# A third raw buffer for the weights' maxima, the last head's sums on another engine, a weight tile rounded one stage earlier, and a new order in the first head

## Chip, cores, metric

One core of one Trainium2 chip. The time is device microseconds of one execution, the median over runs. Engines: TensorE (PE), VectorE (DVE), ScalarE (ACT), GpSimd (POOL), and SyncE (SP), whose queue issues all DMAs here.

## What is computed

A gated layer of two parts. The first ("mixer") adds to x a convolution over the sequence of the products of a context with itself, times the LayerNorm of x. The second is a feed-forward net of two linear layers whose operands are rounded to 8-bit integers with one exponent per block of 32.

```python
def xattn(k, v, q, ssm_kernel, D):           # k = v = the context, q = layernorm(x); head_dim 8, 64 heads
    kv = einsum('bhil,bhjl->bijhl', k_, v_)
    y = irfft(rfft(kv, 2 * L) * rfft(ssm_kernel, 2 * L))[..., :L]
    return einsum('bijhl,bhil->bjhl', y + kv * D, q_)

def mx_quant(x):                             # blocks of 32 along the contraction
    scale = exp2(floor(log2(amax)) - 6)
    return clip(round(xb / scale), -128, 127) * scale

def ffn(x):                                  # weights W1 (4096 x 1024), W2 (1024 x 4096)
    h = bf16(layernorm(bf16(x)) * w + b)
    h = gelu(bf16(mx_quant(h) @ mx_quant(W1).T + b1))
    return bf16(bf16(x) + bf16(mx_quant(h) @ mx_quant(W2).T + b2))

x = x + tanh(g_xattn) * xattn(ctx, ctx, layernorm(x), ssm_kernel, D)
x = x + tanh(g_ffn) * ffn(layernorm(x))
```

x is 8 x 512 x 1024: 32 tiles of 128 rows by 1024.

## The kernel before

The program has two blocks, one behind the other, with all engines meeting between them: `mixer_block` and `ffn_block`. Every order is written out by hand, engine by engine; semaphores tie them.

**First stage.** It runs over 64 heads, two to a tile (`TILE_HEADS`). For a head, ACT copies k (`copy_k`), writes its squares (`squares`) and the upper part of the products in reduced precision (`high_half`, kk_hi); DVE makes the products (`make_kk`) and the rest (`low_half`, kk_lo). TensorE convolves in stretches (`conv_stretch`, L307) with slabs of the taps, which SP loads for each head from a scratch in memory. At the start of a head TensorE waits for kk_lo of that head. DVE multiplies the result with q (`times_q`, in two parts, three instructions each); POOL sums the products in seven adds (`sum_part`, L709 to L721). Once per tile TensorE turns the sums back (`turn_back`, L340), DVE adds x (`residual`, L621), and SP stores the tile (`store_x1`). In the other direction ACT normalises x (`ln_apply`), TensorE turns it (`turn_q`, L320) and ACT takes it (`take_q`).

Between these, DVE takes the maxima of blocks of both weights (`weight_maxima`, L579): 32 tiles of 1 MB, one in each of the first heads, then in alternate heads, and from head 21 on three in two heads (`maxima_heads`). They are loaded by `load_w` into two raw buffers. From head 35 on DVE rounds the second layer's weights (`layer2_ints`, `layer2_clip`, `layer2_quant`) and SP stores them. In the heads between, the first four tiles of the second stage are prepared (`early_*`).

At its end SP waits for all its stores, the last tile's too, before the block ends (L286 to L288).

**Second stage.** The 16 tiles of W1 are loaded (`load_raw`, four buffers; tile 0 is already loaded by `first_loads`), and DVE rounds each in four steps: `weight_ints` (L1159 conversion, L1161 scale), `weight_clip` (L1166), `weight_quant` (L1171). Each releases one bank of the first layer on TensorE (`layer1`, L922). The tiles of x go in groups of two (g): first layer, bias on ACT (`add_bias`, L981), gelu (L988), the rounding of the hidden values on DVE (`peak`, `hidden_*`), second layer (`layer2`, L937), then `second_bias` (L1139, L1142) and `gated_sum` (L1148) on DVE and the store. Banks of group 1 begin eleven banks behind those of group 0. ACT's queue holds `first_norm` of group g + 2 ahead of `add_bias` of group g + 1, and `norm_again` within it, which waits for a tile of x that SP reloads (`reload`) behind the store of the tile before.

## Time and profile before

| what | us |
|---|---|
| median of 3 runs | 2006.51 (2004.93 to 2008.56) |
| the profiled execution, its own time | 2008.35 |
| its span | 2006.4 |
| TensorE busy | 1904.8 (95%) |
| DVE busy | 1694.4 (84%) |
| POOL busy | 962.3 (48%), nearly all in the first stage |
| ACT busy | 755.7 (38%) |

The span is what the rows below measure; the execution's own time holds 1.95 us more around it. Times in the rows are microseconds from the span's start. The stages change near 1028 to 1054 us.

### The profile page before, as it was taken

To read this page: it belongs to the slowest core of one execution; us is meant where nothing else is said; L and a number is where in the kernel's file an instruction comes from. 1 tells how busy PE (TensorE), PEld (TensorE's weight loads), DVE (VectorE), ACT (ScalarE), POOL (GpSimd) and SP (SyncE) were. 2 spreads that over 40 slices of the span, in tenths; PEclk is the share of its full clock that TensorE was granted. 3 is DMA by queue.
4 is the path that set the end of the run, shared out by engine and by line. 5 is a ranking of instruction groups with operands and counts; after the bars stand their busy time and mean duration, and the time that the engine had idled before them with its cause. 6 is when DMAs were issued, how large, how long until landed. Compare 5 with 4: busy or idle time off the path is not lost. (4 is left out here: it accounts for less than half of the span.)

```text
span 2006.4 us, 29505 instructions
## 1 busy us (share of the span) xinstructions
PE 1904.8 (95%) x11680; PEld 1499.5 (75%) x11680; DVE 1694.4 (84%) x2075; ACT 755.7 (38%) x1036; POOL 962.3 (48%) x1035
## 2 busy tenths in 40 slices
PE   6999999999999999999955969999999999999998
PEld 5988888888888898889843736667676666666673
DVE  6899999998898889898859799888888888898843
ACT  3333333333333433333302604444444444444440
POOL 4888899887899999999960000000000000000000
PEclk9999999999999999999978979999999999999999
DMA  6544545555554655555438411222221212212111
GB/s 245 192 171 155 169 157 181 199 213 213 213 199 137 204 181 171 193 181 195 147 112 327 178 49 58 64 74 74 74 74 64 60 57 74 74 54 64 53 43 74
DMA packets 99274, 271.75 MB, mean 135 GB/s; under 512 B 41472, under 2 KB 41472, under 8 KB 90944
## 3 DMA queue, kind: packets, MB, share of 16 engines
q1 hardware_dynamic: 99136, 269.86, 39.3%
q8 instruction: 92, 1.51, 0.3%
q14 instruction: 46, 0.38, 0.1%
HBM read 218.91 MB, written 42.53 MB: 130 GB/s over the span
## 5 line engine op out<-in xcount | busy, mean ns | idle before, releaser
L307 PE MATMUL y_ps<-kk_hi,slab 128*128 128x352 f32 (+6 forms) x3328 | 896.9, 351 | 15.5 <-issue 10.6
L307 PEld LDWEIGHTS y_ps<-kk_hi,slab 128*128 128x128 f32 x3328 | 595.7, 189 | 85.7 <-issue 12.1
L307 PE MATMUL y_ps<-kk_lo,slab 128*128 128x512 f32 (+6 forms) x1664 | 580.7, 349 | 0.0
L937 PE MATMUL acc_ps<-w_T,arena 128*128 128x512 bf16 x2048 | 444.5, 379 | 0.0
L922 PE MATMUL l_ps<-f_xq_T,w_T 128*128 128x256 bf16 x3584 | 398.9, 275 | 19.3 <-ACT arena L981 14.7
L922 PEld LDWEIGHTS l_ps<-f_xq_T,w_T 128*128 128x128 bf16 x3584 | 352.8, 99 | 66.3 <-ACT arena L981 15.2
L937 PEld LDWEIGHTS acc_ps<-w_T,arena 128*128 128x128 bf16 x2048 | 200.4, 98 | 238.4
L1221 POOL TENSOR_TENSOR f_rstd<-f_var_eps,f_neg_half 128x1 f32<-128x1 f32 x28 | 15.4, 549 | 707.3 <-DVE f_var_eps L1037 707.3
L307 PEld LDWEIGHTS y_ps<-kk_lo,slab 128*128 128x128 f32 x1664 | 314.1, 189 | 34.4
L981 ACT ACTIVATE arena<-l_ps,f_b 128x256 bf16<-128x256 f32 x512 | 213.7, 474 | 237.8 <-PE l_ps L922 232.8
L495 DVE TENSOR_TENSOR upper<-y_ps,q_ext 128x768 f32<-128x768 f32 (+1 forms) x128 | 155.8, 1217 | 79.8 <-PE y_ps L307 74.2
L709 POOL TENSOR_TENSOR lsum<-lower 128x240 f32<-128x240 f32 (+1 forms) x128 | 159.1, 1243 | 73.2 <-DVE lower L501 73.1
L367 ACT COPY k_ps<-k_ext 128x512 f32<-128x512 f32 x64 | 37.8, 591 | 412.6 <-DVE kk L475 405.1
L710 POOL TENSOR_TENSOR upper<-upper 128x384 f32<-128x384 f32 (+1 forms) x128 | 185.2, 1447 | 0.0
L481 DVE TENSOR_TENSOR kk_lo<-kk,kk_hi 128x2304 fp32r<-128x2304 f32 x64 | 174.1, 2721 | 10.6 <-ACT kk_hi L381 10.1
L721 POOL TENSOR_TENSOR mixed<-upper 128x192 f32<-128x192 f32 (+1 forms) x128 | 168.7, 1318 | 18.6 <-POOL upper L718 0.4
L381 ACT CAST kk_hi<-kk 128x2304 fp32r<-128x2304 f32 x64 | 136.2, 2128 | 7.9 <-DVE kk L475 5.9
L962 ACT ACTIVATE f_n<-arena,f_shift,f_rstd 128x1024 bf16<-128x1024 f32 x28 | 34.6, 1240 | 247.8 <-POOL f_shift L1223 247.8
L988 ACT ACTIVATE arena<-arena 128x2048 bf16<-128x2048 bf16 x64 | 122.0, 1911 | 0.5
L501 DVE TENSOR_TENSOR lower<-y_ps,q_ext 128x576 f32<-128x576 f32 (+1 forms) x128 | 121.0, 945 | 0.0
L712 POOL TENSOR_TENSOR lsum<-lsum,lower 128x240 f32<-128x240 f32 (+1 forms) x128 | 120.4, 941 | 0.0
L472 DVE TENSOR_TENSOR kk<-k_ps,k_ext 128x1536 f32<-128x1536 f32 x64 | 111.6, 1744 | 0.0
(125 smaller groups left out, 2062.7 us busy)
## 6 DMA issues: line engine op xcount, KB each, us to landing
slab<-taps_scratch SPq DMA_DIRECT2D x128, 512.0 KB, 4.8
arena<-in_w_m SPq DMA_DIRECT2D x32, 1024.0 KB, 6.4
arena<-x_scratch SPq DMA_DIRECT2D x60, 512.0 KB, 4.0
k_ext<-in_ctx_e SPq DMA_DIRECT2D x64, 384.0 KB, 3.5
arena<-in_w SPq DMA_DIRECT2D x17, 1024.0 KB, 7.1
x_tile<-in_x_t SPq DMA_DIRECT2D x32, 512.0 KB, 6.3
x_scratch<-x SPq DMA_DIRECT2D x32, 512.0 KB, 4.5
out_t<-arena SPq DMA_DIRECT2D x32, 512.0 KB, 2.6
```

The costliest lines, as they stand in the source:

```text
L307: mm = nc.tensor.matmul(y_ps[:, y_base + begin:y_base + end], slab[s][:, half, d * P:(d + 1) * P], kk_part[s][:, begin - d * PAIR:end - d ...
L381: nc.scalar.copy(kk_hi[h % 2][:], kk[:].rearrange("p n c -> p (n c)")).then_inc(hi_ready, 1)
L481: nc.vector.tensor_tensor(kk_lo[h % 2][:], kk[:].rearrange("p n c -> p (n c)"), kk_hi[h % 2][:].bitcast(F32), ALU.subtract).then_inc(lo_re ...
L495: nc.vector.tensor_tensor(view(up, 0, [((DIAG + 1) * CH, count), (CH, DIAG), (1, CH)]), view(y_ps, y_at, [(PAIR, count), (CH, DIAG), (1, C ...
L501: nc.vector.tensor_tensor(view(low, B, [(3 * ACCW, count), (ACCW + B, 3), (1, CH)]), view(y_ps, y_at + CH, [(PAIR, count), (CH, 3), (1, CH)]),
L709: add(lsum[:, :, B:], low[:, :, 0, B:], low[:, :, 1, B:], ALU.add).then_inc(lower_two, 1)
L710: add(up[:, :, 0:2, :], up[:, :, 0:2, :], up[:, :, 2:4, :], ALU.add).then_inc(upper_two, 1)
L721: add(out, rows[0], rows[4], ALU.add).then_inc(sums_ready, 1)
L922: mm = nc.tensor.matmul(l1_ps[bank % L1_BANKS][:, a, :], w1_T[:, b, k, a * P:(a + 1) * P], inputs[:, k, :], start=(k == 0), stop=(k == L / ...
L937: mm = nc.tensor.matmul(acc_ps[s][:, c * 512:(c + 1) * 512], hidden[g % 2][:, k, s * P:(s + 1) * P], w2_T[:, k, c * 512:(c + 1) * 512], st ...
L981: done = nc.scalar.activation(hidden[g % 2][:, c, :], l1_ps[bank % L1_BANKS][:, a, :], ACT.Identity, bias=b1_c[:, c:c + 1])
L988: nc.scalar.activation(h, h, ACT.Gelu_apprx_tanh).then_inc(gelu_ready, 1)
```

## The change

It has five parts.

1. Maxima: from the thirteenth tile on, three raw buffers in turn (`maxima_slot`). The third is the one that held the LayerNorm's weights for the early tiles; its first load is issued in head 20 and waits until the early inputs are done.
2. The last head's second part is summed on DVE (`last_part`, the same seven adds), and POOL's call is gone.
3. Tile 0 of W1 is converted and clipped on DVE in the first stage (`first_ints`), behind those sums and ahead of the last residual. Tile 1 is loaded in the first stage too. The second stage begins with tile 0's scale and last step; the scale's instruction moves behind `weight_quant` of the tile before.
4. The last two stores of the first stage (the last tile of x, now kept in the arena, and the last tile of W2) count on a semaphore of their own, which SP awaits in the second stage before it reads them back, and ACT before it writes over their source.
5. First head: ACT writes the squares and kk_hi before it normalises the first tile, DVE makes the products before its statistics, and TensorE turns the first q behind the first stretch. In the second stage, `second_bias(0)` and `gated_sum(0)` move ahead of `peak(1, 1)`, and the loads of tiles 4 and 5 each wait for the bank that frees their place only.

```diff
     maxima_of = [[n for n in range(2 * W_TILES) if maxima_heads[n] == h] for h in range(heads)]
     scales_head = maxima_heads[-1] + 1
+    maxima_slot = [n % 2 if n < 12 else (n - 12) % 3 for n in range(2 * W_TILES)]
     spread_heads = [scales_head + 2 + scales_head % 2 + 2 * i for i in range(4)]
     w2_heads = heads - scales_head - 1
...
-        w_raw = [raw_weights(arena, 2), raw_weights(arena, 3)]
-        w2_raw = w_raw + [raw_weights(arena, 0)]
+        w_raw = w2_raw = [raw_weights(arena, i) for i in (2, 3, 0)]
+        x1_last = raw_weights(arena, 2)[:, L:2 * L]
...
             def load_w(n):
-                if n >= 2:
-                    sp.wait_ge(w_max_ready, n - 1)
-                sp.dma_start(w_raw[n % 2], w_m[n]).then_inc(w_loaded[n % 2], 16)
+                slot = maxima_slot[n]
+                users = [m for m in range(n) if maxima_slot[m] == slot]
+                if users:
+                    sp.wait_ge(w_max_ready, users[-1] + 1)
+                elif slot == 2:
+                    sp.wait_ge(e_input, EARLY)
+                sp.dma_start(w_raw[slot], w_m[n]).then_inc(w_loaded[slot], 16)
 
...
-                    sp.wait_ge(e_input, EARLY)
+                if j < 3:
+                    sp.wait_ge(w_max_ready, 2 * W_TILES)
                 else:
...
+                done = last_stored if j == W_TILES - 1 else w2_stored[j % 3]
                 sp.wait_ge(w2_quant, j + 1)
-                sp.dma_start(w2_q[j], w2_raw[j % 3][:, 0:L].bitcast(BF16)).then_inc(w2_stored[j % 3], 16)
+                sp.dma_start(w2_q[j], w2_raw[j % 3][:, 0:L].bitcast(BF16)).then_inc(done, 16)
...
+                if t == tiles - 1:
+                    sp.dma_start(x1_t[t], x1_last).then_inc(last_stored, 16)
+                else:
+                    sp.dma_start(x1_t[t], x1[t % 2][:]).then_inc(x1_stored[t % 2], 16)
...
+                if h == early_heads + 4:
+                    load_w(14)
                 for n in maxima_of[h - 1] if h >= 1 else []:
-                    if n + 2 < 2 * W_TILES:
-                        load_w(n + 2)
+                    for m in range(n + 1, 2 * W_TILES):
+                        if maxima_slot[m] == maxima_slot[n]:
+                            load_w(m)
+                            break
...
-            for parity in range(2):
-                sp.wait_ge(x1_stored[parity], 16 * (tiles // 2 - 1))
-            sp.wait_ge(w2_stored[2], 16 * (W_TILES // 3))
+            for j in (1, 2):
+                sp.wait_ge(w2_stored[j], 16 * (W_TILES // 3))
             first_loads(sp)
             store_w2(quant_of[heads - 1])
-            store_x1(tiles - 1)
             for i, stored in enumerate(w2_stored):
-                sp.wait_ge(stored, 16 * len(range(i, W_TILES, 3)))
+                sp.wait_ge(stored, 16 * len(range(i, W_TILES - 1, 3)))
             for turned in e_turned:
                 sp.wait_ge(turned, 16 * EARLY // 2)
             for parity in range(2):
-                sp.wait_ge(x1_stored[parity], 16 * (tiles // 2))
+                sp.wait_ge(x1_stored[parity], 16 * ((tiles - 1 + 1 - parity) // 2))
+            store_x1(tiles - 1)
...
-                pe.wait_ge(sums_ready, 2 * TILE_HEADS * (t + 1))
+                pe.wait_ge(sums_ready, min(2 * TILE_HEADS * (t + 1), 2 * heads - 1))
+                if t == tiles - 1:
+                    pe.wait_ge(last_sums, 1)
...
-            turn_q(0)
             for h in range(heads):
                 t = h // TILE_HEADS
                 for i in range(len(stretches)):
                     conv_stretch(h, i)
+                    if h == 0 and i == 0:
+                        turn_q(0)
...
             copy_k(0)
+            squares(0)
+            high_half(0)
             ln_apply(0)
             copy_k(1)
-            squares(0)
-            high_half(0)
             take_q(0)
...
+            def last_part():
+                first, count = PARTS[1]
+                up, low, lsum = upper[1], lower[1], lsums[1]
+                rows = [up[:, :, d, :] for d in range(DIAG + 1)]
+                add = nc.vector.tensor_tensor
+                dve.wait_ge(sums_ready, 2 * heads - 2)
+                dve.wait_ge(products_ready, 2 * heads)
+                add(lsum[:, :, B:], low[:, :, 0, B:], low[:, :, 1, B:], ALU.add).then_inc(last_added, 1)
...
+                add(rows[0], rows[0], rows[1], ALU.add).then_inc(last_added, 1)
...
+                dve.wait_ge(last_added, 6)
+                part = (heads - 1) % TILE_HEADS
+                add(mixed[(tiles - 1) % 2][:, first:first + count, part * CH:(part + 1) * CH], rows[0], rows[4],
+                    ALU.add).then_inc(last_sums, 1)
...
-                if t >= 2:
+                if 2 <= t < tiles - 1:
...
+                out = x1_last if t == tiles - 1 else x1[t % 2][:]
+                nc.vector.tensor_tensor(out.rearrange("p (i k) -> p i k", i=QB),
...
+            make_kk(0)
             ln_stats(0)
-            make_kk(0)
             low_half(0)
...
             times_q(heads - 1, 1)
+            last_part()
+            first_ints(dve)
             residual(tiles - 1)
...
                 sum_part(h, 0)
-            sum_part(heads - 1, 1)
...
-                    sp.wait_ge(l1_ready, 2 * banks)
+                    sp.wait_ge(l1_ready, number(u, banks - 1) + 1)
...
-                if j > W_SLOTS:
+                if j >= 2 + W_SLOTS:
                     sp.wait_ge(w_scaled, j - W_SLOTS + 1)
-                sp.dma_start(w[(j - 1) % W_SLOTS], w1_t[j]).then_inc(w_loaded[1 + (j - 1) % W_SLOTS], 16)
-
-            load_raw(1)
+                sp.dma_start(w[(j - 2) % W_SLOTS], w1_t[j]).then_inc(w_loaded[2 + (j - 2) % W_SLOTS], 16)
...
             load_raw(2)
+            load_raw(3)
...
-            for j in range(5, W_TILES):
+            for j in range(6, W_TILES):
                 load_raw(j)
+            sp.wait_ge(last_stored, 32)
...
                 if b == 0:
+                    if g == 1:
+                        act.wait_ge(last_stored, 32)
...
-                raw = raw_weights(arena, 0) if j == 0 else w[(j - 1) % W_SLOTS]
-                if j == 0:
-                    dve.wait_ge(w_loaded[0], 16)
+                raw = raw_weights(arena, 3) if j == 1 else w[(j - 2) % W_SLOTS]
+                if j == 1:
+                    dve.wait_ge(w_loaded[1], 16)
                 else:
-                    dve.wait_ge(w_loaded[1 + (j - 1) % W_SLOTS], 16 * ((j - 1) // W_SLOTS + 1))
+                    dve.wait_ge(w_loaded[2 + (j - 2) % W_SLOTS], 16 * ((j - 2) // W_SLOTS + 1))
...
-            weight_ints(0)
-            weight_clip(0)
+            weight_scales(0)
+            weight_quant(0)
             for j in range(1, W_TILES):
                 weight_ints(j)
-                weight_quant(j - 1)
+                if j >= 2:
+                    weight_quant(j - 1)
+                weight_scales(j)
                 weight_clip(j)
...
                         quantise_input(GROUP * (g + 1) + s)
                     if g >= 2 and s == 0:
                         gated_sum(GROUP * (g - 2) + 1)
+                    if g == 1 and s == 1:
+                        second_bias(0)
+                        gated_sum(0)
                     if 1 <= g < groups:
                         peak(g, s)
...
-                if 1 <= g <= groups:
+                if 2 <= g <= groups:
                     second_bias(GROUP * (g - 1))
                     gated_sum(GROUP * (g - 1))
...
         def first_loads(sp):
-            sp.dma_start(raw_weights(arena, 0), w1_t[0]).then_inc(w_loaded[0], 16)
+            for j, slot in ((0, 0), (1, 3)):
+                sp.dma_start(raw_weights(arena, slot), w1_t[j]).then_inc(w_loaded[j], 16)
+
+        def first_ints(dve):
+            dve.wait_ge(w_loaded[0], 16)
+            nc.vector.tensor_tensor(first_wq.rearrange("p (k o) -> p k o", o=2 * P),
+                                    raw_weights(arena, 0).rearrange("p (k o) -> p k o", o=2 * P),
+                                    view(raw_weights(arena, 1).bitcast(BF16), 0, [(0, L // P), (1, 2 * P)]),
+                                    ALU.mult).then_inc(w_scaled, 1)
+            dve.wait_ge(w_scaled, 1)
+            nc.vector.tensor_scalar(first_wq, first_wq, 127.0, None, ALU.min).then_inc(ints_ready, 1)
```

ACT at the program's start, before (`kk` and `kk_hi` are head 0's products, `xn` the normalised first tile):

```order
L361 ACTIVATE gate_tanh<-gate 64x1
L367 COPY k_ps<-k_ext 128x512
L395 ACTIVATE shift<-neg_mean,rstd 128x1
L399 ACTIVATE xn<-x_tile,shift,rstd 128x1024
L367 COPY k_ps<-k_ext 128x512
L374 ACTIVATE kk<-k_ext 128x8x64
L381 CAST kk_hi<-kk 128x2304
```

And after:

```order
L375 ACTIVATE gate_tanh<-gate 64x1
L381 COPY k_ps<-k_ext 128x512
L388 ACTIVATE kk<-k_ext 128x8x64
L395 CAST kk_hi<-kk 128x2304
L409 ACTIVATE shift<-neg_mean,rstd 128x1
L413 ACTIVATE xn<-x_tile,shift,rstd 128x1024
L381 COPY k_ps<-k_ext 128x512
```

The squares and kk_hi moved ahead of the normalisation and of the second head's copy.

DVE where the stages change, before (`lower` ends the last products, `x_1` is the last residual, L1159 to L1171 round the weights):

```order
L501 TENSOR_TENSOR lower<-y_ps,q_ext 128x5x3x64
L621 TENSOR_TENSOR x_1<-turn_ps,x_tile 128x1024
L96 UNCONDITIONAL_BRANCH
L1021 UNCONDITIONAL_BRANCH
L1159 TENSOR_TENSOR arena<-arena 128x2048
L1161 TENSOR_SCALAR w_scale<-arena 128x256
L1166 TENSOR_SCALAR arena<-arena 128x2048
L1159 TENSOR_TENSOR f_o_res<-w_T,arena 128x2048
```

And after, from the first of the moved adds on:

```order
L539 TENSOR_TENSOR lsum<-lower 128x5x80
L540 TENSOR_TENSOR upper<-upper 128x5x128
L542 TENSOR_TENSOR lsum<-lsum,lower 128x5x80
L544 TENSOR_TENSOR upper<-upper 128x5x64
L546 TENSOR_TENSOR upper<-upper,lsum 128x5x64
L548 TENSOR_TENSOR upper<-upper,lsum 128x5x24
L551 TENSOR_TENSOR mixed<-upper 128x5x64
L1307 TENSOR_TENSOR arena<-arena 128x2048
L1312 TENSOR_SCALAR arena<-arena 128x2048
L658 TENSOR_TENSOR arena<-turn_ps,x_tile 128x1024
L97 UNCONDITIONAL_BRANCH
```

Seven adds and two steps of the rounding stand between the last products and the last residual.

DVE in group 1 of the second stage, after, where the last step of tile 5's input (L1124) is followed by the moved part (L1180 to L1189) and the peaks (L1134 on):

```order
L1124 TENSOR_TENSOR f_hq<-f_hq,f_scale_x 128x1024
L1180 TENSOR_TENSOR f_o_res<-acc_ps,b_b 128x1024
L1183 TENSOR_TENSOR f_o_res<-f_o_res 128x1024
L1189 SCALAR_TENSOR_TENSOR arena<-f_o_res,f_gate_tanh,arena 128x1024
L1134 TENSOR_SCALAR f_weighted<-arena 128x2048
```

Before, the same three stood behind the first statistics of tiles 6 and 7.

## Rows read from the trace of the kernel before

**Rows 1.** The page's first part: engine, busy us, share of span, instructions.

```profile
PE 1904.8 (95%) x11680; PEld 1499.5 (75%) x11680; DVE 1694.4 (84%) x2075; ACT 755.7 (38%) x1036; POOL 962.3 (48%) x1035
```

**Rows 2.** Timeline of the start: start us, us, engine, line, instruction [idle before <-releaser].

```profile
13.09 1.94 PE L320 MATMUL turn_ps<-ident,xn 128*128 128x128 f32 x8 [13.09 <-ACT xn L399]
16.23 2.56 DVE L481 TENSOR_TENSOR kk_lo<-kk,kk_hi 128x2304 fp32r<-128x2304 f32 x1 [4.52 <-ACT kk_hi L381]
18.93 0.63 PE L307 MATMUL y_ps<-kk_hi,slab 128*128 128x352 f32 x1 [3.90 <-DVE kk_lo L481]
```

**Rows 3.** DMA issues of 12 to 12.9, then 12.5 to 13.0: KB each, us to landing.

```profile
slab<-taps_scratch SPq DMA_DIRECT2D x1, 512.0 KB, 3.7
slab<-taps_scratch SPq DMA_DIRECT2D x2, 512.0 KB, 4.7
```

**Rows 4.** Timeline of PE: one later group of the same transposes.

```profile
963.09 1.04 PE L320 MATMUL turn_ps<-ident,xn 128*128 128x128 f32 x8
```

**Rows 5.** Timeline of PE: first products of heads it came late to.

```profile
379.19 0.40 PE L307 MATMUL y_ps<-kk_hi,slab 128*128 128x352 f32 x1 [0.69 <-issue]
411.60 0.40 PE L307 MATMUL y_ps<-kk_hi,slab 128*128 128x352 f32 x1 [1.37 <-issue]
...
542.61 0.40 PE L307 MATMUL y_ps<-kk_hi,slab 128*128 128x352 f32 x1 [1.72 <-issue]
```

**Rows 6.** Waits: who waited for whom: us in total, times, longest.

```profile
DVE w_max L579 <- DMA arena<-in_w_m: 19.8, 11, 4.4
```

**Rows 7.** Timeline of DVE: a late maximum and the next kk_lo.

```profile
495.22 2.29 DVE L579 TENSOR_REDUCE w_max<-arena 128x64 f32<-128x2048 f32 x1 [2.63 <-DMA arena<-in_w_m]
...
505.86 2.70 DVE L481 TENSOR_TENSOR kk_lo<-kk,kk_hi 128x2304 fp32r<-128x2304 f32 x1
```

**Rows 8.** Timelines of DVE, POOL, PE and SP where the stages change.

```profile
1022.71 0.35 DVE L498 TENSOR_TENSOR upper<-y_ps,q_ext 128x192 f32<-128x192 f32 x1
...
1029.89 1.15 DVE L501 TENSOR_TENSOR lower<-y_ps,q_ext 128x960 f32<-128x960 f32 x1
1031.12 1.03 POOL L709 TENSOR_TENSOR lsum<-lower 128x400 f32<-128x400 f32 x1 [0.52 <-DVE lower L501]
...
1037.71 1.97 PE L340 MATMUL turn_ps<-ident,mixed 128*128 128x128 f32 x8 [9.66 <-POOL mixed L721]
1039.72 1.23 DVE L621 TENSOR_TENSOR x<-turn_ps,x_tile 128x1024 f32<-128x1024 f32 x1 [8.68 <-PE turn_ps L340]
1040.97 0.32 SPq L230 DMA_DIRECT2D x_scratch<-x  x1
1044.07 0.81 SPq L868 DMA_DIRECT2D w_T<-in_w  x2
1046.44 0.68 DVE L1166 TENSOR_SCALAR arena<-arena 128x2048 int16<-128x2048 int16 x1
1050.40 2.29 DVE L1159 TENSOR_TENSOR f_o_res<-w_T,arena 128x2048 int16<-128x2048 f32 x1 [3.27 <-DMA w_T<-in_w]
...
1054.48 2.28 DVE L1159 TENSOR_TENSOR arena<-w_T,arena 128x2048 int16<-128x2048 f32 x1
```

**Rows 9.** Waits of SP at the end of the first stage (L288).

```profile
SPq L288 <- DMA x_scratch<-x: 2.1, 1, 2.1
```

**Rows 10.** The chain that ended last, in the second stage: start us, us, what.

```profile
1103.39 38.61 PE l_ps L922 x336
```

**Rows 11.** Timelines of DVE, ACT and PE at the restart in the second stage.

```profile
1194.29 1.22 DVE L1139 TENSOR_TENSOR f_o_res<-acc_ps,b_b 128x1024 bf16<-128x1024 f32 x1
1197.54 0.69 DVE L1024 BATCH_NORM_STATS2 f_stats<-f_n 128x6 f32<-128x512 bf16 x1
...
1204.47 1.24 ACT L970 ACTIVATE f_o_res<-arena,f_shift,f_rstd 128x1024 bf16<-128x1024 f32 x1 [5.73 <-DMA arena<-x_scratch]
...
1197.33 8.11 PE L922 MATMUL l_ps<-f_xq_T,w_T 128*128 128x256 bf16 x48 [13.62 <-ACT arena L981]
1206.49 15.89 PE L922 MATMUL l_ps<-f_xq_T,w_T 128*128 128x256 bf16 x144 [1.05 <-ACT arena L981]
```

More of the change, by code:

```diff
@@ L71, in mixer_block @@
 def mixer_block(nc, x_t, ctx_e, taps_in, skip_in, g_x, scratch, x1_t, w_m, w2_t, w2_q, ln_w, ln_b, arena, w_inv, rs, shift1,
-                first_loads, tiles):
+                first_loads, last_stored, first_ints, tiles):
     heads = tiles * TILE_HEADS
@@ L161, in mixer_block @@
         k_loaded = [sem("k_loaded0"), sem("k_loaded1")]
-        w_loaded = [sem("w_raw_loaded0"), sem("w_raw_loaded1")]
+        w_loaded = [sem(f"w_m_loaded{i}") for i in range(3)]
         w_max_ready, w_floor, w_bits, w_inv_ready = sem("w_max_ready"), sem("w_floor"), sem("w_bits"), sem("w_inv_ready")
@@ L883, in _ @@
             for i in range(W_SLOTS):
-                last = [j for j in range(1, W_TILES) if (j - 1) % W_SLOTS == i][-1]
+                last = [j for j in range(2, W_TILES) if (j - 2) % W_SLOTS == i][-1]
                 sp.wait_ge(w_scaled, last + 1)
```

41 lines of the change are left out of this document (25 added, 16 removed).

## The prediction

> **What bounds the kernel now.** I read the page's busy shares first, then the chain of work that ended last, then the waits, and last the timeline at the places where TensorE stands still. TensorE is busy for 1904.8 of the 2006.4 us span [rows 1], so an edit counts only as far as it shortens one of TensorE's gaps or makes one. The reader should see four kinds of gap: the start, before the first head; short stalls at head starts in the stage where the weights' maxima are taken; the change of stage near 1028 to 1054 us; and the restart after the first second-layer products, near 1197 us. Elsewhere TensorE runs without a break, and a gain made before such a stretch is carried through it.
>
> **The start.** Before, TensorE turns the first q (8 transposes at 13.09 us, in time that is idle anyway) and begins the first head at 18.93, right behind kk_lo, which DVE ended at 16.23 + 2.56 = 18.79 [rows 2]. ACT's new order moves kk_hi ahead of the LayerNorm, so kk_lo is done some 3.7 us earlier (about 15.0). But the second half of the first slab is what is late next: the two halves are issued at about 12.5 and 13.0; the first takes 3.7 us to land and the median of both is 4.7 [rows 3], so the second takes 5.7 and lands at 18.7. The store of taps_lo that releases it isn't moved. So the reorder gains 0.1 us. The transposes now stand behind the first stretch of head 0, on TensorE's path: one such group costs at most 1.04 us [rows 4]. ACT's take_q then comes near 25 us, and its first reader, times_q of head 0, starts only near 29, so it waits for nothing new. Clock: the group at 13.09 took 1.94 us against 1.04 later [rows 2, 4], and the first product of head 0 took 0.63 us where the same form takes 0.40 [rows 2, 5], so both ran at the lower level. Whether the early transposes helped the clock rise sooner in head 0 the trace can't tell; if they did, their absence costs up to 1 us more. I take +1.0 us, ends -0.2 and +2.0.
>
> The Trainium skill, "TensorE: Matmul & The Clock Gate", section "Part 4: PE-mode transpose", says that such transposes don't count as TensorE activity for the clock. By that rule the start costs +0.9, by the other reading up to +2.0; the row at 18.93 still being slow agrees with the rule but doesn't prove it.
>
> **The maxima.** DVE waits 11 times, 19.8 us in all, for the raw weight tiles [rows 6]. From head 21 on an odd head takes two maxima and an even head one, with two buffers. The pattern: at 495.22 DVE has waited 2.63 us for the second tile; from the end of that maximum (497.5) to the end of the next kk_lo (505.86 + 2.70 = 508.56) it needs 11.1 us [rows 7], and TensorE's next head waits for exactly that, starting at 508.66. TensorE's stalls of this kind are 1.37, 1.22, 1.10, 1.50, 0.93 and 1.72 us; the first and the last are shown, six in all [rows 5]. Sum 7.84. With a third buffer the tile for the second maximum is asked for one maximum earlier; it is then issued some 18 us before use, where the late ones landed 5 to 10 us after issue. Without the wait kk_lo is 1.2 us ahead of TensorE here: TensorE's own head ends at 508.66 - 1.50 = 507.2 (its stall is one of the six), and kk_lo would end at 508.56 - 2.63 = 505.9. What stays is the stall of 0.69 at 379.19, which has no DMA wait in front of it [rows 5]. The extra load (tile 14, issued in head 20) stands in SP's queue behind a wait for head 18's work, which is over. I take -7.8 us; ends -6.5 (one stall stays) and -8.5 (0.69 goes too).
>
> **The change of stage.** Before: DVE's last products end at 1029.89 + 1.15 = 1031.04; POOL sums them from 1031.12; TensorE turns the result at 1037.71 (1.97 us); DVE adds the residual at 1039.72 (1.23 us); SP stores at 1040.97, and the next stage's first DMA goes out at 1044.07 [rows 8]. SP's wait there is 2.1 us for that store [rows 9].
> - Last sums on DVE: seven adds of 400, 640, 400, 320, 320, 120 and 320 elements. The nearest rows are DVE's fp32 products, 192 elements in 0.35 and 960 in 1.15 us [rows 8], so 0.15 + 1.04 per thousand elements. That is 3.7 us one by one, and 3.3 with neighbours overlapping. Ends: 2.6 (elements alone) and 6.6 (no faster than POOL). The sums end at 1034.3.
> - The tile rounded early: 2.29 us (the conversion at 1050.40) and 0.68 [rows 8]. It now stands ahead of the residual on DVE, with the whole path queued behind it. TensorE's transposes (1.97) hide two thirds: sums end 1034.3, rounding ends 1037.3, residual ends 1038.5. The tile itself was asked for within the last head, so no wait.
> - Store not awaited: SP issues it (about 0.3) and leaves at 1038.9. What the stage's end costs beside the wait is 1044.07 - 1040.97 - 0.3 - 2.1 = 0.7 at most, 0.5 by the gap behind the landing. Next stage at 1039.4, 4.7 us earlier.
> - In the next stage the first tile needed from a new DMA is tile 2 instead of tile 1. Before, tile 1 landed at 1050.40, 6.3 us after its issue, and tile 2's conversion began at 1054.48 [rows 8]. Now tile 2's begins at 1039.4 + 6.3 = 1045.7. Gain 8.7 us. The store of 512 KB is now in flight beside it; it can cost from 0 to 1.3 us. The second raw tile had 1.5 us in hand before, and keeps it.
> From there DVE sets the pace, tile by tile, and TensorE after it, without a stall from 1103.39 [rows 10]; both move as a whole. I take -8.7 us; ends -9.5 and -5.5.
>
> **The restart.** second_bias(0) and gated_sum(0) move ahead of peak(1,1). They fill DVE from 1194.29 to 1197.54, 3.25 us [rows 11]. Ahead of them stood the first statistics of tiles 6 and 7, which release POOL, then ACT's first_norm, and behind that in ACT's queue the add_bias that TensorE waits for. So TensorE restarts at 1197.33 + 3.25. In return the store and reload for norm_again(1) come early, and the wait of ACT at 1204.47 (5.73 us) and TensorE's 1.05 us at 1206.49 are gone [rows 11]. Net 3.25 - 1.05 = +2.2 us; ends 0 and +3.3. The early loads of tiles 4 and 5 gain nothing, since ACT is still in its four gelus when they would be used.
>
> **Sum.** +1.0 - 7.8 - 8.7 + 2.2 = -13.3 us. The profiled execution took 2008.35 us (span 2006.4 and 1.95 around it): 1995.0 by its own measure. It lies 1.8 above the median of the three runs, 2006.51, against which the forecast is 1993.2.
>
> **Rivals.**
> - *The restart is free* (12%). For it: the clock is low after the gap (48 products in 8.11 us against 144 in 15.89 [rows 11]), and a later start might meet a rise of it sooner. Against: the gap before it only grows. -15.5: 1991.0.
> - *The stage's end waits for the store after all* (10%): the end of a block might hold until DMAs are through, whatever SP waits for. For it: the trace shows no block left with a store in flight. Then the next stage starts 2.1 us later: -11.2, 1995.3.
> - *DVE's own work holds the heads* (7%): two maxima take 4.5 us with no wait, and 379.19 shows a stall without one [rows 5]. For it: only 1.2 us in hand. If all six stalls stay: -5.5, 2001.0.
> - *Slower: TensorE's clock stays low in the stretch from 1103.39* (4%). Its 336 products take 38.61 us [rows 10]; at the lower level each costs up to 0.11 us more (15.89 / 144, twice) [rows 11]. It decides from 13.3 / 0.11 = 121 products, a third of them; with all it is +37 - 13 = +24, 2030. Against: before, the clock rises within this stretch, and its work is the same.
> The Trainium skill, same page, section "HAM oscillation — how this bites in real kernels", says that bursts with waits between them keep dropping the clock; TensorE's banks at one per tile conversion are such bursts. By it the banks there would stay slow as they partly do now, hidden behind DVE.
>
> **How the numbers follow.** The forecast has 67%. Its terms' ends reach from -18.2 to -6.7 (1988.3 to 1999.8) if all fall alike, which they don't, so 1989.0 to 1998.5; that takes in the first two rivals and leaves out the other two and a few per cent of tails. A measurement of this kernel can tell about 0.2%, 4 us, from no change. Faster by more: 93%; within: 3% (part of the third rival); slower: 4%.
>
> **What would show it.** In the changed profile: TensorE's first product still near 18.8, and its eight transposes between the first and second stretch of head 0; no wait of DVE for the weight tiles and none of the six stalls, but the one of 0.69; seven adds on DVE in about 3.3 us; the first DMA of the second stage less than 1 us behind the last residual; the second tile conversion of a newly loaded tile about 8.7 us earlier than the rest of the shift explains; TensorE's restart gap longer by about 3 us, with no stall of 1.05 behind it. The prediction fails if the first head starts well before 18, if kk_lo still comes last at head starts, or if the stage's end waits.

## The result, and the profile after

The changed kernel takes 1993.5 us (median of four runs, 1993.12 to 1994.17) against 2007.53 for the kernel before in the same session (2004.93 to 2009.1): ratio 0.9935, 95% interval 0.992 to 0.995. The forecast was 1993.2. Against the 2006.51 of the first three runs, from which the forecast counts, that is -13.0 us where -13.3 was forecast; against the 2007.53 of the same session it is -14.0. The profiled executions differ by more, 2006.4 to 1991.2 us of span, -15.2: the one of before lies 0.8 above its median, the one of after 0.4 below its own.

Busy time hardly moved (answers to [rows 1]):

```profile
PE 1900.2 (95%) x11632; PEld 1499.2 (75%) x11680; DVE 1695.3 (85%) x2082; ACT 755.8 (38%) x1036; POOL 955.9 (48%) x1028
```

**The start** (answers to [rows 2]). Timeline: start us, us, engine, line, instruction, [idle before <-releaser].

```profile
12.49 2.56 DVE L495 TENSOR_TENSOR kk_lo<-kk,kk_hi 128x2304 fp32r<-128x2304 f32 x1 [0.62 <-ACT kk_hi L395]
18.38 0.63 PE L318 MATMUL y_ps<-kk_hi,slab 128*128 128x352 f32 x1 [18.38 <-DMA slab<-taps_scratch]
23.77 1.03 PE L331 MATMUL turn_ps<-ident,xn 128*128 128x128 f32 x8
```

kk_lo ends at 15.05 and the slab is the last to come, at 18.38, 0.55 earlier than before's first product. The transposes stand behind the first stretch and take 1.03, of which 0.9 us show up on TensorE's path. By the second q (46.90 in this kernel, 46.34 before) TensorE is 0.56 us behind before.

**The heads.** TensorE turns the sums back once per tile. The first three rows are before, the next three after:

```profile
383.01 1.03 PE L340 MATMUL turn_ps<-ident,mixed 128*128 128x128 f32 x8
415.46 1.04 PE L340 MATMUL turn_ps<-ident,mixed 128*128 128x128 f32 x8
447.76 1.04 PE L340 MATMUL turn_ps<-ident,mixed 128*128 128x128 f32 x8
```

```profile
382.92 1.04 PE L353 MATMUL turn_ps<-ident,mixed 128*128 128x128 f32 x8
413.79 1.03 PE L353 MATMUL turn_ps<-ident,mixed 128*128 128x128 f32 x8
444.65 1.03 PE L353 MATMUL turn_ps<-ident,mixed 128*128 128x128 f32 x8
```

A tile takes 30.87 us after. Before, it took 32.45 and 32.30, with stalls of 1.37 and 1.22 in them [rows 5]. All six stalls and all of DVE's waits for the raw tiles of the maxima [rows 6] are gone; the stall of 0.69 is still there at 379.11, with 0.63.

**The change of stage** (answers to [rows 8]):

```profile
1020.42 1.15 DVE L515 TENSOR_TENSOR lower<-y_ps,q_ext 128x960 f32<-128x960 f32 x1
...
1024.51 0.49 DVE L551 TENSOR_TENSOR mixed<-upper 128x320 f32<-128x320 f32 x1
1024.92 2.28 DVE L1307 TENSOR_TENSOR arena<-arena 128x2048 int16<-128x2048 f32 x1
1025.10 1.94 PE L353 MATMUL turn_ps<-ident,mixed 128*128 128x128 f32 x8 [6.52 <-issue]
1027.23 0.69 DVE L1312 TENSOR_SCALAR arena<-arena 128x2048 int16<-128x2048 int16 x1
1027.84 1.22 DVE L658 TENSOR_TENSOR arena<-turn_ps,x_tile 128x1024 f32<-128x1024 f32 x1
1029.16 0.33 SPq L236 DMA_DIRECT2D x_scratch<-arena  x1
1029.90 0.89 SPq L906 DMA_DIRECT2D w_T<-in_w  x2
1029.93 0.23 DVE L1203 TENSOR_SCALAR w_scale<-arena 128x256 uint16<-128x256 uint16 x1 [0.87 <-PEq L97]
...
1036.52 2.29 DVE L1199 TENSOR_TENSOR arena<-w_T,arena 128x2048 int16<-128x2048 f32 x1 [2.15 <-DMA w_T<-in_w]
```

The next stage's first load goes out 0.74 us behind the last store's issue. From the last products to the conversion of tile 2 it is 16.10 us, before 1054.48 - 1029.89 = 24.59 [rows 8].

**The restart** (answers to [rows 10, 11]):

```profile
1085.31 39.20 PE L961 MATMUL l_ps<-arena,w_T 128*128 128x256 bf16 x336 [3.96 <-DVE w_T L1213]
1156.81 9.58 PE L961 MATMUL l_ps<-f_xq_T,w_T 128*128 128x256 bf16 x64 [4.67 <-issue]
1183.12 24.06 PE L961 MATMUL l_ps<-f_xq_T,w_T 128*128 128x256 bf16 x192 [16.72 <-ACT arena L1022]
```

The gap grew from 13.62 to 16.72, and the stall of 1.05 is gone. From the 64 products to the end of the 192 it is 50.37 us, before 48.09. From there to the end it is 784.0 us in both traces.

### The profile page after: what moved, and what is told of

It is laid out like the page before. It is cut to its first block and busy times, and to the rows that moved or that the text cites. A ratio compares the mean times of both kernels' runs of the same rounds, so it can differ in the third digit from the quotient of the medians.

```text
span 1991.2 us, 29456 instructions
## 1 busy us (share of the span) xinstructions
PE 1900.2 (95%) x11632; PEld 1499.2 (75%) x11680; DVE 1695.3 (85%) x2082; ACT 755.8 (38%) x1036; POOL 955.9 (48%) x1028
## 5 line engine op out<-in xcount | busy, mean ns | idle before, releaser
L976 PE MATMUL acc_ps<-w_T,arena 128*128 128x512 bf16 x2000 | 439.5, 379 | 2.5
L961 PE MATMUL l_ps<-f_xq_T,w_T 128*128 128x256 bf16 x3584 | 399.1, 275 | 21.4 <-ACT arena L1022 16.7
L748 POOL TENSOR_TENSOR lsum<-lower 128x240 f32<-128x240 f32 x127 | 169.1, 1332 | 65.8 <-DVE lower L515 65.6
L749 POOL TENSOR_TENSOR upper<-upper 128x384 f32<-128x384 f32 x127 | 183.5, 1445 | 0.0
L760 POOL TENSOR_TENSOR mixed<-upper 128x192 f32<-128x192 f32 x127 | 158.4, 1247 | 18.5 <-POOL upper L757 0.4
L751 POOL TENSOR_TENSOR lsum<-lsum,lower 128x240 f32<-128x240 f32 x127 | 119.0, 937 | 0.0
```

Source lines behind the costliest of these rows:

```text
L748: add(lsum[:, :, B:], low[:, :, 0, B:], low[:, :, 1, B:], ALU.add).then_inc(lower_two, 1)
L749: add(up[:, :, 0:2, :], up[:, :, 0:2, :], up[:, :, 2:4, :], ALU.add).then_inc(upper_two, 1)
L760: add(out, rows[0], rows[4], ALU.add).then_inc(sums_ready, 1)
L961: mm = nc.tensor.matmul(l1_ps[bank % L1_BANKS][:, a, :], w1_T[:, b, k, a * P:(a + 1) * P], inputs[:, k, :], start=(k == 0), stop=(k == L / ...
L976: mm = nc.tensor.matmul(acc_ps[s][:, c * 512:(c + 1) * 512], hidden[g % 2][:, k, s * P:(s + 1) * P], w2_T[:, k, c * 512:(c + 1) * 512], st ...
```

## Experiments

Single profiled executions differ from each other by 1 to 3 us for reasons that have nothing to do with an edit (a DMA's landing, the clock behind a stall, both below). So where a term of 1 to 3 us is at stake, the distance between two rows near it is compared, and the medians beside it. The changed kernel's median, 1993.5, is from another session than those of the experiments. The kernel before ran in every session, with medians from 2006.24 to 2007.53, so a difference from 1993.5 is good to about 1 us.

### 1. The third buffer alone

The kernel before, with part 1 of the diff only (`maxima_slot`, `load_w`, the load of tile 14).

> The kernel before with the third raw buffer alone. Theory A (the six stalls are nearly all of it, and each costs about 0.2 us more than the idle time shown, since the changed kernel gained 9.1 us between 379 and 603 us where 7.84 had been summed): 9.1 us less than before, some 1998.4; the stage's last products near 1020.8 instead of 1029.9; no wait of DVE for the raw tiles. Theory B (the sum as predicted): 7.8 us less. Rival (DVE's own work holds the heads, the gain came from other parts): 0 to 2 us less, with stalls at head starts between 411 and 543.

1999.04 us against 2007.19 of before, ratio 0.9957 (0.9942 to 0.9971); span 1996.9, 9.5 less than before's. DVE's last products:

```profile
1020.34 1.15 DVE L507 TENSOR_TENSOR lower<-y_ps,q_ext 128x960 f32<-128x960 f32 x1
```

That is 9.55 earlier than before [rows 8], and DVE's waits for the maxima's raw tiles are gone. The rival (DVE's own work holds the heads) is out. The median alone, -8.2, can't tell 7.8 from 9.1; the tile periods can: in the kernel before, the five periods that hold the six stalls (383.01 to 546.43) were together 9.07 us longer than 5 x 30.87, for 7.84 of idle shown. Each stall costs about 0.2 more than its idle.

### 2. The restart's order back

```diff
-                    if g == 1 and s == 1:
-                        second_bias(0)
-                        gated_sum(0)
...
-                if 2 <= g <= groups:
+                if 1 <= g <= groups:
```

> The changed kernel, with second_bias(0) and gated_sum(0) put back behind the first statistics of tiles 6 and 7. Theory: the 3.2 us that they fill on DVE leave the path before the restart, and the stall of 1.05 behind it comes back: 2.1 us less than the changed kernel, 1991.4; TensorE's gap before its restart 13.6 instead of 16.7. Rival (the early store and reload bring something later that the profile doesn't show yet): no less, 1993.5 or more.

1990.57 us, ratio to before 0.9916 (0.9901 to 0.9931): 2.9 less than the changed kernel.

```profile
1155.60 9.63 PE L961 MATMUL l_ps<-f_xq_T,w_T 128*128 128x256 bf16 x64 [4.70 <-issue]
1178.63 8.32 PE L961 MATMUL l_ps<-f_xq_T,w_T 128*128 128x256 bf16 x48 [13.39 <-ACT arena L1022]
1187.78 15.89 PE L961 MATMUL l_ps<-f_xq_T,w_T 128*128 128x256 bf16 x144 [0.83 <-ACT arena L1022]
```

Gap and stall are those of before, and the stretch from the 64 products to the end of the 192 is 1203.67 - 1155.60 = 48.07, 2.30 less than in the changed kernel. So this part of the change costs 2.3 us, and nothing behind it gives it back.

### 3. The last store awaited

```diff
             store_x1(tiles - 1)
+            sp.wait_ge(last_stored, 32)
```

> The changed kernel, with SP waiting for the last two stores before the first stage ends. Theory: the stage's end moves by the store's time, 2.1 to 2.4 us, and all behind it: 1995.8; the time from the store's issue to the next stage's first DMA 3.1 instead of 0.74. Rival (the next stage's first load was slowed by the stores in flight and gets back what it loses): 0 to 1 us more.

1995.14 us, ratio 0.994 (0.9924 to 0.9957): 1.6 more than the changed kernel.

```profile
1028.56 0.33 SPq L236 DMA_DIRECT2D x_scratch<-arena  x1
1031.62 0.33 SPq L907 DMA_DIRECT2D w_T<-in_w  x1
...
1037.90 2.29 DVE L1200 TENSOR_TENSOR arena<-w_T,arena 128x2048 int16<-128x2048 f32 x1 [1.82 <-DMA w_T<-in_w]
```

From store to first load it is 3.06 instead of 0.74 us, 2.32 more. From that issue to the conversion of tile 2 it is 6.28 us, 6.62 in the changed kernel, so 2.0 us arrive. Whether the store in flight costs the load this 0.34 can't be told: with the same store in flight it was 5.1 us in experiment 11 and 7.2 in experiment 4. In the changed kernel the end of the block didn't wait for a store that no engine awaits.

### 4. The first q turned first

```diff
+            turn_q(0)
             for h in range(heads):
...
-                    if h == 0 and i == 0:
-                        turn_q(0)
```

> The changed kernel, with TensorE's eight transposes of the first tile ahead of head 0's first stretch, as before; ACT's and DVE's new order kept. Theory: xn is there at 15.2, the transposes run until 17.1 in idle time, the slab lands at 18.4 and head 0 starts with it: 1.05 us less than the changed kernel, 1992.4; times_q of head 0 at 28.3 instead of 29.35. Rival (transposes just ahead change when the clock rises in the first stretch): up to 1 us more or less than that. If the transposes delay head 0 past 18.4: less gain by as much.

1991.94 us, ratio 0.9919 (0.9904 to 0.9934), 1.6 less than the changed kernel.

```profile
15.33 1.94 PE L331 MATMUL turn_ps<-ident,xn 128*128 128x128 f32 x8 [15.33 <-ACT xn L412]
17.71 0.66 PE L318 MATMUL y_ps<-kk_hi,slab 128*128 128x352 f32 x1 [0.45 <-DMA slab<-taps_scratch]
...
19.78 0.33 PE L318 MATMUL y_ps<-kk_lo,slab 128*128 128x352 f32 x1
```

By the second q TensorE is 2.2 us ahead of the changed kernel: 0.67 since the slab landed earlier in this run, 0.9 for the transposes, and 0.7 since the products reach 0.33 us, the higher level of the clock, at 19.78 instead of 22.09. (The level is read from the durations here: the profile's clock column says 1.00 for the whole start, also where products take twice as long. The same eight transposes take 1.94 us here and behind the stall at 600.58 below, where the column says 0.50.) So about 1.5 us are the edit's, where 1.05 was expected. TensorE keeps 2.1 until 600.58, and there loses 1.5 of it:

```profile
600.58 1.94 PE L353 MATMUL turn_ps<-ident,mixed 128*128 128x128 f32 x8 [3.03 <-issue]
...
604.45 1.05 PE L318 MATMUL y_ps<-kk_hi,slab 128*128 128x512 f32 x2
```

Two such products take 0.62 at the higher level. Behind this stall of 3.0 us, which every kernel here has but those of experiments 8, 10 and 12, the clock falls in some executions and not in others: from this turn to the next q's it was 11.4 us here (granted clock 0.50 from 600 to 606), 9.9 in the changed kernel (0.51 from 602 to 604, 0.63 from there to 606), 8.6 in experiment 3 (1.00 throughout), and 8.55 without the stall. It fell in eight of the eleven kernels with the stall, one execution each.

### 5. The last sums on POOL

```diff
-                pe.wait_ge(sums_ready, min(2 * TILE_HEADS * (t + 1), 2 * heads - 1))
-                if t == tiles - 1:
-                    pe.wait_ge(last_sums, 1)
+                pe.wait_ge(sums_ready, 2 * TILE_HEADS * (t + 1))
...
-            last_part()
+            dve.wait_ge(w2_quant, W_TILES)
             first_ints(dve)
...
                 sum_part(h, 0)
+            sum_part(heads - 1, 1)
```

> The changed kernel, with the last head's second part summed on POOL again, and the first tile's rounding running on DVE beside it. Theory: POOL needs 6.6 us from the last products to the turn, as before, against 3.5 on DVE, but the rounding (3.0 us, of which 1.0 stood on the path) is then hidden: residual's end 9.9 us behind the last products instead of 7.5, so 2.4 us more than the changed kernel, 1995.9. Ends: 0 if POOL's adds are shorter than they seemed, 3.6 if DVE's rounding stretches them. Rival (the move to DVE gained nothing, since the next stage waits for something else): no more than 1993.5.

1998.47 us, ratio 0.996 (0.9945 to 0.9975): 5.0 more than the changed kernel, above the upper end of 3.6 that was expected.

```profile
1021.79 1.15 DVE L513 TENSOR_TENSOR lower<-y_ps,q_ext 128x960 f32<-128x960 f32 x1
1022.86 2.28 DVE L1306 TENSOR_TENSOR arena<-arena 128x2048 int16<-128x2048 f32 x1
1023.02 3.00 POOL L746 TENSOR_TENSOR lsum<-lower 128x400 f32<-128x400 f32 x1 [0.82 <-DVE lower L513]
1025.17 1.40 DVE L1311 TENSOR_SCALAR arena<-arena 128x2048 int16<-128x2048 int16 x1
1025.98 1.98 POOL L747 TENSOR_TENSOR upper<-upper 128x640 f32<-128x640 f32 x1
...
1032.03 1.97 PE L351 MATMUL turn_ps<-ident,mixed 128*128 128x128 f32 x8 [12.08 <-POOL mixed L758]
```

The same add took 1.03 us before, when DVE stood still [rows 8]. Here DVE's conversion runs beside it, and it takes 3.00; the next takes 1.98 beside the clip, and the clip itself 1.40 instead of 0.69. POOL's seven adds take 9.0 instead of 6.5 us. So most of DVE's rounding wasn't hidden behind POOL but added to it: 2.4 of its 3.0 us. From the last products to the conversion of tile 2 it is 21.4 us (that one begins at 1043.19), 5.3 more than in the changed kernel, about 0.5 of it by a slower load of tile 2. The Trainium skill, "GPSIMD Engine Reference", section "1. Specifications", has GpSimd's SBUF interfaces contend with DVE instructions that have two SBUF inputs; this trace agrees, with 3.00 against 1.03.

### 6. The first rounding in the second stage

```diff
             last_part()
-            first_ints(dve)
             residual(tiles - 1)
...
+            weight_ints(0)
             weight_scales(0)
+            weight_clip(0)
             weight_quant(0)
```

> The changed kernel, with tile 0 converted and clipped in the second stage instead of ahead of the last residual; its loads and the last sums stay. Theory: the residual, the store and the next stage's first loads come 1.0 us earlier; the 3.0 us of rounding then fall into DVE's wait for tile 2 (2.15 us) and that 1.0. The conversion of tile 2 comes 0.2 us earlier to 0.8 later behind the last products, so 0 to 0.8 us more or less than the changed kernel, 1993.5. Rival (the early rounding carries its part of the 8.5 us gained at the stage's change): 2 to 3 us more, 1996.

1991.38 us, ratio 0.9928 (0.9913 to 0.9943): 2.1 less than the changed kernel by the medians.

```profile
1019.93 1.15 DVE L515 TENSOR_TENSOR lower<-y_ps,q_ext 128x960 f32<-128x960 f32 x1
...
1026.58 1.23 DVE L658 TENSOR_TENSOR arena<-turn_ps,x_tile 128x1024 f32<-128x1024 f32 x1 [2.08 <-PE turn_ps L353]
1028.68 2.29 DVE L1198 TENSOR_TENSOR arena<-arena 128x2048 int16<-128x2048 f32 x1 [0.87 <-PEq L97]
...
1035.90 2.29 DVE L1198 TENSOR_TENSOR arena<-w_T,arena 128x2048 int16<-128x2048 f32 x1
```

From the last products to the conversion of tile 2 it is 15.97 us, 0.13 less than in the changed kernel; the wait of 2.15 for tile 2 is gone, filled by tile 0. Bank 11 of group 0 follows at the same distance. So rounding tile 0 one stage early is worth nothing, within 0.2 us of rows. The 2.2 us by which its profiled span is shorter stand elsewhere: 0.5 were there by the last products already, and the 192 products behind the restart took 22.42 us instead of 24.06, by the clock.

### 7. The norms behind the biases, in group 2

The restart's wait is TensorE's longest in the second stage, and the change made it longer. TensorE needs a free bank, ACT frees it, and ACT stands at `first_norm` of tile 6, whose statistics DVE takes at 1176.71. So the order in ACT's queue was changed.

```diff
                         if b in (4, 8, 12):
                             gelu(g, b // 4 - 1)
+                        if g == 2 and b == 8:
+                            first_norm(GROUP * 3)
+                            first_norm(GROUP * 3 + 1)
...
-                    if g + 2 < groups:
+                    if g != 1 and g + 2 < groups:
                         first_norm(GROUP * (g + 2) + s)
```

> The changed kernel, with ACT's first_norm of tiles 6 and 7 moved behind the bias of bank 8 of group 2, instead of ahead of group 2's first bias. Theory: TensorE's restart needs only free banks, and ACT doesn't give them since it waits for DVE's first statistics; with the order changed the gap of 16.7 us closes, and the 256 products behind it run at the higher clock (0.11 us each, 28 us, where they took 33.6): 17 to 21 us less than the changed kernel, about 1975. Rival (DVE, which has lost no work, is late for group 3's input or hidden values): the gap moves behind the next second-layer products, gain 0 to 8 us.

1986.64 us, ratio 0.9903 (0.9887 to 0.992): 6.9 less than the changed kernel. That is the rival's size; its reason, that DVE is late, experiment 9 puts to the test.

```profile
1158.26 25.40 PE L962 MATMUL l_ps<-f_xq_T,w_T 128*128 128x256 bf16 x208 [4.68 <-issue]
1184.55 5.42 PE L962 MATMUL l_ps<-f_xq_T,w_T 128*128 128x256 bf16 x48 [0.90 <-ACT arena L1023]
...
1231.31 7.27 PE L962 MATMUL l_ps<-f_xq_T,w_T 128*128 128x256 bf16 x48 [6.73 <-ACT arena L1023]
1240.29 15.89 PE L962 MATMUL l_ps<-f_xq_T,w_T 128*128 128x256 bf16 x144 [1.70 <-ACT arena L1023]
```

The gap of 16.7 us closed, and 8.4 us of gap came up one group later, at the same place of ACT's queue: first_norm of tile 8 at 1227.61, and norm_again of tile 3 at 1238.27, which waits for its reload.

### 8. The inverses kept first

```diff
+                if h in spread_heads:
+                    keep_inverses(spread_heads.index(h))
                 if t + 1 < tiles:
                     if h % TILE_HEADS == 0:
                         ln_apply(t + 1)
...
-                if h in spread_heads:
-                    keep_inverses(spread_heads.index(h))
```

> The changed kernel, with ACT's keep_inverses ahead of ln_apply in the four heads that spread the inverses. Theory: TensorE's stall of 3.0 us at 602.66 waits for that copy, which stands in ACT's queue behind a LayerNorm whose rstd comes late from POOL; it goes with its 0.2 us of restart, and the clock no longer drops behind it (0 to 2.9 us, by the 8.6 to 11.4 us that the next piece took in different runs, 8.4 undisturbed): 3.2 to 6 us less than the changed kernel, about 1989. Rival (POOL's late sums hold the turn themselves): the stall stays within 0.5 us, 1993.

1987.94 us, ratio 0.9907 (0.9892 to 0.9922): 5.6 less than the changed kernel.

```profile
600.15 1.03 PE L353 MATMUL turn_ps<-ident,mixed 128*128 128x128 f32 x8
```

The stall of 3.0 is gone (the turn stands right behind the products ahead of it), and from those products to the next q TensorE has gained 4.55 us: 3.17 for the stall and 1.38 for the clock that no longer falls behind it.

### 9. The norms behind the biases in every group

Experiment 7 with `if b == 8 and g + 1 < groups`, the norms left ahead only at g == 0, and

```diff
-                        if b == 2:
+                        if b == 10:
                             norm_again(GROUP * (g - 2) + 1)
```

> The changed kernel, with ACT's first_norm of the next group behind the bias of bank 8 in every group, and norm_again of the odd tile behind bank 10 instead of 2. Theory: with group 2 alone TensorE had gained 18.5 us by the second-layer products at 1190, and lost 10 of them again in group 3, where the same two waits of ACT stand (first_norm of tile 8 until 1227.6, norm_again of tile 3 until 1238.3). With both out of the way the whole 18 us stay: 1975. Rival (DVE, busy 47 of 55 us a group, is itself the bound here and what is gained comes back at group 3 or 4): 1983 to 1987, as with group 2 alone.

1974.4 us, ratio 0.9842 (0.9826 to 0.9859): 19.1 less than the changed kernel.

```profile
1157.00 25.29 PE L961 MATMUL l_ps<-f_xq_T,w_T 128*128 128x256 bf16 x208 [4.69 <-issue]
1183.29 5.41 PE L961 MATMUL l_ps<-f_xq_T,w_T 128*128 128x256 bf16 x48 [1.00 <-ACT arena L1022]
1188.75 27.57 PE L976 MATMUL acc_ps<-w_T,arena 128*128 128x512 bf16 x125
1216.16 28.11 PE L961 MATMUL l_ps<-f_xq_T,w_T 128*128 128x256 bf16 x256
```

Nothing comes back: TensorE has no gap in group 3 any more, and is 18.5 us ahead at its second-layer products (1188.75 against 1207.23). DVE wasn't the bound; the order of ACT's queue was. Two waits of ACT were moved at once here, the norms and norm_again; what each is worth alone wasn't measured.

### 10. All three reorders

Experiments 9, 8 and 4 in one kernel.

> The same kernel, with the first q turned first, and with keep_inverses ahead of ln_apply. Theory: the three places are independent, so the gains add: 1993.5 - 18 (this reordering) - 4.6 (the inverses) - 2.2 (the first q, which was lost again at the stall of 602 us when tried alone, by the clock) = 1968.7. Rival (they meet one wait): at least 3 us short of the sum, 1972 or more.

1969.32 us, ratio 0.9814 (0.98 to 0.9829). That is 0.6 above the sum expected from rows. The medians of the three single edits would add up to 1967.3, 2.0 lower, within what three differences across sessions allow; the rival's 3 us of shortfall didn't come.

### 11. The first q turned twice

The transposes ahead of the first stretch, sixteen instead of eight; the second eight write the same values again.

```diff
-                for n in range(LB):
+                for n in range(2 * LB if t == 0 else LB):
+                    n %= LB
```

> The changed kernel, with TensorE's transposes of the first q ahead of the first stretch, and done twice over (16 instead of 8, the same result). They run from 15.3 to about 19.2 and hold the first product back by some 1.4 us. Theory 1 (transposes count for the clock): the first fast product comes within 1 us of the first product, near 19.5; with 8 transposes it came 1.9 us behind it, without any just ahead 2.8 to 3.4. Theory 2 (they don't count): 2.8 to 3.4 us behind it, near 22.

One execution: 1987.12 us.

```profile
15.49 3.46 PE L332 MATMUL turn_ps<-ident,xn 128*128 128x128 f32 x16 [15.49 <-ACT xn L413]
18.71 0.41 PE L318 MATMUL y_ps<-kk_hi,slab 128*128 128x352 f32 x1
18.95 0.32 PE L318 MATMUL y_ps<-kk_lo,slab 128*128 128x352 f32 x1
```

The first product runs at the higher level, and only transposes ran on TensorE before it. In the eight kernels without transposes ahead, the first product took 0.63, and the higher level came 3.0 (experiment 3) to 5.9 us (experiment 5) behind it. Against experiment 4 the second group of transposes gains nothing by the second q (44.78 and 44.68), since it holds the first product back by 1.0. The span is 6.0 us shorter than that of the changed kernel: 2.1 by the second q, 1.35 by the clock behind the stall at 600 us, 1.5 by a faster load of tile 2, and the rest in the second stage. Only the first of these is the edit's: 1.6 by the clock and 0.9 for the transposes, less 0.3 for the later first product.

### 12. All three reorders, and q twice

> The kernel with all three reorders, and the first q's eight transposes done twice over, ahead of the first stretch. Theory (transposes raise the clock, as the run before showed, and then it is up when the slab lands): the first stretch's products run at the higher level from the first on, also where the slab lands late; 1.5 to 2.8 us less than with the three reorders alone: 1967. Rival (that run's early rise was chance, or the second group holds the first product back by more than the clock gives): 1969 to 1971, and slow products behind the first.

1966.89 us, ratio 0.9798 (0.9782 to 0.9814), the fastest kernel of this study. Its median is 2.4 below that of experiment 10, but from another session, and the intervals of the two ratios overlap (0.98 to 0.9829 there).

```profile
15.26 3.64 PE L332 MATMUL turn_ps<-ident,xn 128*128 128x128 f32 x16 [15.26 <-ACT xn L413]
18.56 0.64 PE L318 MATMUL y_ps<-kk_hi,slab 128*128 128x352 f32 x1
...
19.84 0.32 PE L318 MATMUL y_ps<-kk_lo,slab 128*128 128x352 f32 x1
```

The clock rises 1.3 us behind the first product here, not before it: the time, 1966.9 where 1967 was expected, came as forecast, but the theory's picture (all products at the higher level from the first on) didn't. In the two profiled executions this kernel is 2.4 us ahead of experiment 10's by the second q (45.22 and 47.59): 0.4 since the slab landed later there (19.00), and 2.0 since the clock rose 5.65 us behind the first product there. How much of the difference of the medians is the edit's, one such pair can't tell.

## Why the prediction held, point by point

Terms in us of profiled span, by the distances between rows that stand above.

| term | predicted | measured |
|---|---|---|
| start | +1.0 | +0.56 |
| the six stalls of the maxima | -7.8 | -9.1 |
| other places in the first stage | 0 | -0.95 |
| change of stage | -8.7 | -8.5 |
| banks and the stretch behind them | 0 | +0.5 |
| restart | +2.2 | +2.3 |
| sum | -13.3 | -15.2 |

- **Start: right mechanism, and a size that one execution can't confirm.** The slab took the place of kk_lo as the last to come, as said. Its issue came 0.37 earlier (12.17 instead of 12.54), which is chance: the store of taps_lo that releases it stood where it had stood (8.10 and 8.05), and in the fourteen traces the issue came 3.7 to 4.9 us behind that store. The transposes cost 0.9 of the 1.04, and the clock, which rose 3.7 us behind the first product instead of 3.0, another 0.2. In the eight kernels with this order the second q stands between 46.07 and 47.94, before it stood at 46.34: this term's noise is larger than the term.
- **The start and the rule on transposes.** From the Trainium skill, "TensorE: Matmul & The Clock Gate", section "Part 4: PE-mode transpose", the prediction weighed the rule that transposes don't raise the clock, at +0.9 against +2.0, and took the row at 18.93 as in keeping with it. Experiments 4, 11 and 12 speak against the rule for the transposes here: with them right ahead the first row at the higher level came 0.2 to 2.1 us behind the first product, and without any 3.0 to 5.9. In the kernel before (and in experiment 1), an idle 3.9 us stood between them, and it came 3.0 us behind, as if there had been none. In experiment 10, with 1.86 us idle between, it came 5.65 behind; what a gap does isn't settled here. Nor is it shown what the transposes were worth in the kernel before, since the spread without any is as large as the effect.
- **Maxima: the mis-sized term.** All six stalls went, and the one of 0.69 stayed, as the step said. The step summed the idle time shown. Idle is counted from the modelled end of the last product, but its successor would have started before that end: products of this kind start 0.16 apart and last 0.32. So each stall was 0.2 us dearer than shown. That the overlap is the reason is argued from these spacings; the 0.2 itself is measured.
- **Other places.** A further small stall of 0.28, at 363.76, went too, with 0.5 us, also in experiment 1. The prediction put nothing down for it. 0.3 is the clock behind the stall of 3.0 us: chance, as experiment 4 shows.
- **Change of stage: right in its steps, one of them worth nothing.** The next stage's first load left 4.7 us earlier counted from the last products, as said (9.48 us behind them instead of 14.18). The sums on DVE took 3.3 us, as said too; what they save against undisturbed POOL is, by experiment 6, 1026.58 - 1019.93 = 6.65 us from products to residual against 9.83 [rows 8], 3.2. The store not awaited brings 2.3. The rest, 3.2 us by experiment 6 (1028.68 to 1035.90, against 1044.10 to 1054.48 [rows 8]), goes with tile 1 being there already; no run takes that alone. The prediction charged the early rounding 1.0 us on the path (measured 0.8: 7.42 us from products to residual with it, 6.65 without) and never asked where else it would fit. Experiment 6 shows that it is a wash: left in the second stage, it fills the 2.15 us that DVE otherwise waits for tile 2.
- **Restart: right.** +2.2 against +2.3, by the changed kernel against before and by experiment 2. Experiment 7 shows that the way it goes, through ACT's norms, is the one the prediction named.
- **The rivals.** "The restart is free" is out (experiment 2), "the stage's end waits" is out (0.74 us, and experiment 3), "DVE's own work holds the heads" is out (experiment 1). The slower clock didn't come: the 336 products took 39.2 us where they had taken 38.6. The banks of 16 products ahead of them took 1.9 to 3.6 us each, as before, hidden behind DVE.
- The sum's error of 1.9 in the profiled span is mostly that of the maxima. That the median came within 0.3 is luck in good part. Counted from the profiled execution of before (2008.35) the forecast was 1995.0, and that of the changed kernel took 1993.12, 1.9 less. But the profiled execution of before lay 1.8 above its median of then, 2006.51, and that of the changed kernel 0.4 below its own; the two offsets cancel the error.

## What to carry to other kernels

In this kernel each stall that the trace shows on TensorE at a head's start cost some 0.2 us more than its idle time; look for the like in yours, and for what the clock does behind it: here a stop of 3 us cost up to 2.9 more. Before filling a wait with work, ask where that work would stand otherwise; and before moving work in front of an engine's next release, follow the release through the other queues: the three instructions moved here cost 2.3 us because ACT's queue held a norm, which waits for DVE's statistics behind them, ahead of the biases. The largest gap was one that the change lengthened, and its cause was the order of two things in one queue; fixing it in one group moved it to the next, fixing it in all of them gave 19 us.

## What the runs showed of the hardware

- TensorE's fp32 transposes can raise its clock: with sixteen of them ahead, and nothing else, the first product ran in 0.41 us instead of 0.63 in one of two executions (experiment 11); in the other (experiment 12) the rise came 1.3 us later. This differs from the Trainium skill, "TensorE: Matmul & The Clock Gate", section "Part 4: PE-mode transpose", unless these transposes don't run in the mode that the page describes, which no row shows; here the measurement decides.
- A stop of 3.0 us, at the same place in kernels that differ elsewhere, was followed by 8.6 to 11.4 us for the same work, as the granted clock stayed at 1.00 or fell to 0.50.
- An add on POOL of 400 elements took 1.03 us with DVE idle and 3.00 beside DVE's conversion, which has two SBUF inputs.
- A block may end with a store in flight: the next block's first DMA left 0.74 us behind its issue, and 3.06 where SP awaited it.
